# Delta rule inputs scaled on GpSimd, with undrained barriers, a later bank wait and two new orders

## The reference

```
x = x + L0 linear attention;   x = x + L0 FFN
x = x + L1 causal attention (16 heads);   x = x + L1 FFN (16 small experts with group routing, one shared)
x = x + L2 gated delta rule;   x = x + L2 FFN (ternary weights, gelu)
x = x + L3 mixer (attention, short convolution, halting steps, top-2 experts);   x = x + L3 FFN (top-2 of 8 experts)
```

```
xp = silu(conv4(x @ in_proj.T) + conv_b)
q = l2norm(xp @ Wq.T per head);  k = l2norm(xp @ Wk.T per head);  v = xp @ Wv.T
alpha, beta = mean over a head of sigmoid(xp @ W.T + b)
```

## Time and profile before

| | us |
|---|---|
| runs, three | 1912.32, 1925.83, 1933.3 |
| median of the runs | 1925.83 |
| profiled execution, device time | 1933.14 |
| its span in the profile | 1931.3 |
| PE busy | 1542.5 (80%) |
| DVE busy | 1153.2 (60%) |
| ACT busy | 849.0 (44%) |
| POOL busy | 569.4 (29%) |

### The profile page before, as it was taken

The page is one execution under the profiler, slowest core; times in us unless marked ns, Lnnn a source line. Parts: engine busy times, 40 slices in busy tenths (PEclk is TensorE's granted clock), DMA queues, the critical chain, the costliest instruction groups (busy, mean ns, idle before and its releaser), DMA issues. The chain is left out here.

```text
span 1931.3 us, 46920 instructions
## 1 busy us (share of the span) xinstructions
PE 1542.5 (80%) x16703; PEld 1135.5 (59%) x16703; DVE 1153.2 (60%) x3234; ACT 849.0 (44%) x1633; POOL 569.4 (29%) x782
## 2 busy tenths in 40 slices
PE   5779799999878887789997868788889589431992
PEld 3646566666455665568886545455555389331992
DVE  5755577777467656545653457687877344464344
ACT  2422355565511114434442325466666378201783
POOL 4111011111111112432220321113333446376464
PEclk9979799999989998889997888699998589755996
DMA  4000222222079500000000100222322044121334
GB/s 180 1 1 1 67 58 56 59 57 59 6 229 325 189 1 1 0 3 3 4 3 2 67 1 1 66 66 73 82 70 61 25 113 132 68 88 43 88 92 149
DMA packets 84685, 125.00 MB, mean 65 GB/s; under 512 B 17328, under 2 KB 70576, under 8 KB 82928
## 3 DMA queue, kind: packets, MB, share of 16 engines
q1 hardware_dynamic: 75824, 104.30, 18.5%
q0 software_dynamic: 8640, 17.78, 2.6%
HBM read 67.47 MB, written 55.59 MB: 64 GB/s over the span
## 5 line engine op out<-in xcount | busy, mean ns | idle before, releaser
L1559 DVE TENSOR_REDUCE small<-ps 128x8 f32<-128x1024 f32 (+1 forms) x256 | 312.0, 1224 | 108.8 <-PE ps L1339 70.4
L1482 ACT ACTIVATE scr<-ps 128x1024 f32<-128x1024 f32 x256 | 262.4, 1025 | 212.1 <-PE ps L1314 120.8
L244 POOL TENSOR_TENSOR rstd<-vare,neghalf 128x4 f32<-128x4 f32 (+1 forms) x72 | 63.3, 879 | 414.2 <-DVE vare L223 413.7
L1352 PE MATMUL ps<-scr 128*32 128x256 f32 x2048 | 171.7, 409 | 0.2 <-ACT scr L1482 0.2
L2906 POOL DMA_INDIRECT results<-scr x142 | 136.4, 960 | 98.1 <-DVE scr L2893 49.8
L1301 PEld LDWEIGHTS ps<-scr_r 32*128 32x128 f32 x1024 | 81.3, 193 | 140.0 <-issue 72.6
L2840 PE MATMUL ps<-scr 128*128 128x128 f32 x1136 | 153.0, 279 | 0.0
L1301 PE MATMUL ps<-scr_r 32*128 32x256 f32 x1024 | 134.7, 341 | 22.7 <-ACT scr L1482 12.5
L1332 PE MATMUL ps<-scr_r 32*128 32x256 f32 x1024 | 136.4, 348 | 10.1 <-DMA scr_r<-scr_r 5.6
L2840 PEld LDWEIGHTS ps<-scr 128*128 128x128 f32 x1136 | 141.6, 196 | 0.0
L2886 DVE TENSOR_TENSOR scr<-ps,scr 128x256 f32<-128x256 f32 x142 | 60.3, 425 | 130.3 <-ACT scr L2877 124.7
(11 more groups left out here) (416 smaller groups left out, 3495.7 us busy)
## 6 DMA issues: line engine op xcount, KB each, us to landing
scr_r<-scr_r SPq DMA_DIRECT2D x512, 64.0 KB
rows_m<-kinds SPq DMA_DIRECT2D x8, 2064.0 KB, 30.1
rows_f<-kinds SPq DMA_DIRECT2D x8, 2064.0 KB, 73.7
scr<-results SPq DMA_DIRECT2D x32, 256.0 KB
scr<-rows_m SPq DMA_DIRECT2D x71, 64.5 KB
scr<-rows_f SPq DMA_DIRECT2D x71, 64.5 KB
scr<-in_l3m SPq DMA_DIRECT2D x1, 3072.0 KB, 9.9
results<-scr POOLq DMA_INDIRECT x142
```

The lines of the kernel that those rows point to most:

```text
L244: pool.tensor_tensor(k.rstd[:, 0:self.J], k.vare[:, 0:self.J], k.neghalf[:, 0:self.J], ALU.pow).then_inc(self.e["rstd_ready"].sem, 1)
L1352: ins = pe.matmul(ps[32 * r:32 * r + 32, 6, col:col + 256], Vp[:, c % 2, 4 * kt + r, at:at + 32], PT[:, g % 2, r, kt * 256:kt * 256 + 256] ...
L1482: act.activation(PT[:, g % 2, 2 * x:2 * x + 2, :], ps[:, 4:6, :], ACT.Exp).then_inc(e["prob_ready"].sem, 1)
L1559: dve.tensor_reduce(nf[:, half, 0:blocks, at:at + 2].rearrange("p q a -> p a q"), ps[:, 2 * (p % 2):2 * (p % 2) + 2, :].rearrange("p a (q ...
```

## The change

GpSimd, not VectorE, scales queries and keys in the delta inputs, right behind its power; the signal `scaled` goes. At the end of four phases (attention with sorting, both sorted experts, `phase_between`) GpSimd increments the barrier's semaphore without a drain. The power in `space` goes. In the routed FFN the wait for bank 6 moves from ahead of gate and up to ahead of the spreading matmuls. The double norm's normalisation, its transposes and their copy come one block later. In linear attention keys and values come ahead of the transposes, on TensorE and on ScalarE.

```diff
--- before.py
+++ after.py
@@ -180,7 +180,11 @@
             if name in ph:
                 ph[name](eng)
             if n < len(self.phases) - 1:
-                eng.drain().then_inc(self.phase_end, 1)
+                if name in ph.get("landed", ()):
+
+                    eng.sem_inc(self.phase_end, 1)
+                else:
+                    eng.drain().then_inc(self.phase_end, 1)
 
                 if name == "sp" and "sp_late" in ph:
                     ph["sp_late"](eng)
@@ -305,7 +309,7 @@
 class TwiceNorm(Norm):
 
 
-    lag = (1, 1, 2)
+    lag = (1, 1, 3)
 
     def __init__(self, k, bank, scale, shift, once):
         super().__init__(k, 4, bank, scale=scale, shift=shift)
@@ -539,10 +543,9 @@
                 sums(it - 1)
             if there(it):
                 queries(it)
+                keys_values(it)
             if there(it - 2):
                 turn(it - 2)
-            if there(it):
-                keys_values(it)
             if there(it - 1):
                 uses(it - 1)
             if there(it - 2):
@@ -564,13 +567,13 @@
         for it in range(NBLK + 3):
             if there(it):
                 feature(it, eq, rq, ps[:, 0, :], "q_ready", "q_read", "phq_ready")
+                four = lambda ap: ap.rearrange("p (b t c) -> p b t c", b=2, t=2)
+                feature(it, four(ek), four(rk), kpart(0), "kv_ready", "k_read", "phk_ready")
             if there(it - 2):
                 wait(act, "o_turned", it - 2)
                 wait(act, "proj_ready", it - 3)
                 act.activation(oT, ps[:, 6, :], ACT.Copy).then_inc(e["oT_kept"].sem, 1)
             if there(it):
-                four = lambda ap: ap.rearrange("p (b t c) -> p b t c", b=2, t=2)
-                feature(it, four(ek), four(rk), kpart(0), "kv_ready", "k_read", "phk_ready")
                 wait(act, "prod_ready", it - 1)
                 act.activation(vb[:, :, 0:128].rearrange("p (b t) c -> p b t c", b=2), kpart(128),
                                ACT.Copy).then_inc(e["v_ready"].sem, 1)
@@ -708,12 +711,6 @@
             else:
                 if begun(it):
                     pe.wait_ge(e["h_ready"].sem, e["h_ready"].at(it - 1, chunks - 1 + c))
-            if c < routed:
-                if c:
-                    pe.wait_ge(e["spread_read"].sem, e["spread_read"].at(it, c))
-                else:
-                    if begun(it):
-                        pe.wait_ge(e["spread_read"].sem, e["spread_read"].at(it - 1))
             x = k.XT[:, bass.ts(it, BLK)]
             s = 2 * (c % 2)
             ins = pe.matmul(ps[:, s, :], gate[:, c * P:(c + 1) * P], x, start=True, stop=True)
@@ -722,6 +719,10 @@
             ins.then_inc(e["gu_ready"].sem, 1)
             if c < routed:
                 pe.wait_ge(e["widened"].sem, e["widened"].at(it, c + 1))
+                if c:
+                    pe.wait_ge(e["spread_read"].sem, e["spread_read"].at(it, c))
+                elif begun(it):
+                    pe.wait_ge(e["spread_read"].sem, e["spread_read"].at(it - 1))
                 for j in range(4):
                     ins = pe.matmul(ps[:, 6, j * P:(j + 1) * P], wide[:, it % 2, c, j * P:(j + 1) * P],
                                     k.w["const"]["ident"], start=True, stop=True)
@@ -765,7 +766,7 @@
                 ln.pe_route(pe, it)
         if lag:
 
-            staged_by((2,), (0,), pe, NBLK, lambda it, stages: body(it, lambda s: stages() if s == 0 else None), late)
+            staged_by((3,), (0,), pe, NBLK, lambda it, stages: body(it, lambda s: stages() if s == 0 else None), late)
         elif routed:
             written_out(pe, NBLK, body, late, 2)
         else:
@@ -811,7 +812,7 @@
         if route:
             route.act(act)
         if lag:
-            staged_by((2,), (0,), act, NBLK, lambda it, stages: body(it, lambda s: stages() if s == 0 else None), late)
+            staged_by((3,), (0,), act, NBLK, lambda it, stages: body(it, lambda s: stages() if s == 0 else None), late)
         else:
             def open_it():
                 act.wait_ge(consts.e["consts_made"].sem, consts.e["consts_made"].at(0))
@@ -1611,7 +1612,7 @@
             sort.share(dve)
 
     front(Opening(project, high, low, heads_out))
-    k.add_phase(pool=pool, pe=pe, act=act, dve=dve, sp=sp)
+    k.add_phase(pool=pool, pe=pe, act=act, dve=dve, sp=sp, landed=("pool",) if sort else ())
 
 
 def conv_taps(dve, c, x, cw, cb):
@@ -1636,7 +1637,7 @@
 
     nc, ps, cst, w = k.nc, k.ps, k.w["const"], k.w["l2a"]
     e = k.signals(NBLK, xp_ready=1, conv_ready=1, conv_gate=1, xc_ready=1, gate_turned=2, gate_kept=2, means_ready=1,
-                  qk_ready=1, squares=1, qk_kept=1, v_ready=1, v_read=1, norms_ready=1, inverse_norms=1, scaled=1)
+                  qk_ready=1, squares=1, qk_kept=1, v_ready=1, v_read=1, norms_ready=1, inverse_norms=1)
     last = k.signals(1, clamped=1, logs=1, log_sums=1)
     c, sg, xc, gt, sq, n2, rn, mean, bias = k.carve(
         (512,), (512,), (2, 512), (2, 512), (1024,), (16,), (16,), (2, 2), (2,))
@@ -1748,8 +1749,12 @@
     def pool(pool):
         for it in range(NBLK):
             wait(pool, "norms_ready", it)
-            wait(pool, "scaled", it - 1)
             pool.tensor_tensor(rn, n2, k.neghalf[:, 0:16], ALU.pow).then_inc(e["inverse_norms"].sem, 1)
+            pool.drain()
+            wait(pool, "qk_kept", it)
+            rows = heads(qkv[:, tl(it), 0:256])
+            pool.tensor_tensor(rows, rows, spread_last(rn, 64).rearrange("p (t b) d -> p t b d", b=4), ALU.mult)
+            pool.drain()
 
     def dve(dve):
 
@@ -1781,13 +1786,6 @@
             dve.drain()
             dve.tensor_scalar(n2, n2, 1e-24, None, ALU.max).then_inc(e["norms_ready"].sem, 1)
 
-        def scale(it):
-            wait(dve, "inverse_norms", it)
-            wait(dve, "qk_kept", it)
-            rows = heads(qkv[:, tl(it), 0:256])
-            dve.tensor_tensor(rows, rows, spread_last(rn, 64).rearrange("p (t b) d -> p t b d", b=4),
-                              ALU.mult).then_inc(e["scaled"].sem, 1)
-
         for it in range(-1, NBLK):
             if there(it + 1):
                 conv(it + 1)
@@ -1795,9 +1793,6 @@
                 sizes(it)
             if there(it + 1):
                 conv_gated(it + 1)
-            if there(it - 1):
-                scale(it - 1)
-        scale(NBLK - 1)
         wait(dve, "means_ready", NBLK - 1)
         dve.tensor_scalar(alpha, ps[:, 6, 0:64].rearrange("p (t h) -> p t h", h=2), 1e-19, None,
                           ALU.max).then_inc(last["clamped"].sem, 1)
@@ -2688,17 +2683,11 @@
         b, e, o = NBLK - 1, self.e, self.once
         pool.wait_ge(e["places"].sem, e["places"].at(b))
         self.send(pool, b, 0)
-        self.space(pool)
         pool.wait_ge(o["second_named"].sem, o["second_named"].at(0))
         for j in range(4):
             t = 4 * b + j
             pool.indirect_dma_start(self.rows, bass.IndirectOffsetOnAxis(ap=self.place[:, 1, t:t + 1], axis=0),
                                     self.twin[:, j, :], None).then_inc(self.sent[2 + b % 2].sem, 16)
-
-    def space(self, pool):
-
-        two = self.k.two
-        pool.tensor_tensor(two[2][:, 0, :], two[1][:, 0, :], self.k.neghalf[:, 0:4], ALU.pow)
 
     def send(self, pool, b, n, tiles=range(4)):
         for t in tiles:
@@ -2908,7 +2897,7 @@
         for j in range(SORTED - OUT, SORTED):
             landed(pool, j)
 
-    k.add_phase(sp=sp, pe=pe, act=act, dve=dve, pool=pool)
+    k.add_phase(sp=sp, pe=pe, act=act, dve=dve, pool=pool, landed=("pool",))
 
 
 class Gathered:
@@ -2995,13 +2984,11 @@
                 pool.wait_ge(d.e["named"].sem, d.e["named"].at(b - 1))
                 d.send(pool, b - 1, 0)
             if 0 <= b - 2 < NBLK:
-                if b == NBLK + 1:
-                    d.space(pool)
                 pool.wait_ge(d.e["second_named"].sem, d.e["second_named"].at(b - 2))
                 d.send(pool, b - 2, 1)
         d.all_sent(pool)
 
-    k.add_phase(sp=sp, dve=dve, pe=pe, act=act, pool=pool)
+    k.add_phase(sp=sp, dve=dve, pe=pe, act=act, pool=pool, landed=("pool",))
 
 
 def phase_last_rows(k, g, out):
```

## The result

The changed kernel takes 1867.39 us (median of 4 runs, 1866.91 to 1869.51), the kernel before 1929.57 us in the 4 runs beside it (1912.32 to 1936.49). The ratio is 0.969, 95% interval 0.963 to 0.976. The forecast was 1869. Beside the experiments the kernel before takes 1926.75 us (e1 to e4: 23 runs, 1917.06 to 1936.03) and, on a second chip, 1929.03 us (e5 to e8: 14 runs, 1920.41 to 1937.89). One run of e3_lag3, 2250.40 us at a granted clock of 0.66, was in a slower state of the chip, and the medians here are of the other runs.

The account below looks back on a forecast made before the run. TensorE, busy 80% of the span, was taken to bound the kernel where it does not wait for other engines. Terms 17.9 + 15.7 + 14.6 + 7.5 + 1.6 = 57.3 took 1933.14 to 1875.8, as median 1868.5, said 1869; range 1852 to 1891.

Parts of the forecast that it names:

- the five places: Barriers, routed FFN, double norm, linear attention, delta rule's inputs: waits on other engines in the first four, no TensorE gap in the last.
- Barriers and spacing power: Four phase ends: bare increments replace GpSimd's drains and the spacing power goes; 17.9 us off, bounds 1 and 19.
- a busy unit: Last phase: if GpSimd is really occupied as long as the drain, its first addition waits 0.8 us; gain 5.0, not 5.84.
- Rival A: Phase ends: the increment queues behind the drain's work, so barriers give 1 us instead of 17.9; 1886, chance 0.12.
- The later bank wait: Routed FFN: gate and up no longer wait for bank 6's read; 15.7 us off, bounds 8 and 19.5.
- The new wait before the third spread: Routed FFN: VectorE late by about 0.5 us at chunk 2, made up before chunk 3.
- Lag 3: Double norm: normalisation one block later ends VectorE's 3.7 us wait for GpSimd's powers, TensorE becomes the bound; 14.6 us off.
- Linear attention: Keys and values ahead of the transposes close gaps of 1.80 and 1.53 us; 7.5 us off, bounds 2 and 9.
- Scaling: Delta inputs: GpSimd scales at 2.54 us, gain only at the stage's end; 1.6 us off, bounds 3 off and 8 on.
- The lower end of the range: Whole kernel: range starts at 1852; upper bounds of gain (19, 17, 16.5, 9, 3) were said to give 1861.

Follow-up runs that it names:

- e1: Kernel before with GpSimd's bare increments at the four phase ends and without the spacing power, nothing else; 1904.28 us, ratio 0.990.
- e4: Kernel before with keys and values ahead of the turned rows on TensorE, key features ahead of the copy on ScalarE; 1920.55 us, ratio 0.995.
- e5: Kernel before with keys and queries scaled on GpSimd behind its power, nothing else; 1925.32 us beside 1929.03, ratio 0.998.
- e8: Changed kernel plus a last scratch phase timing three VectorE forms alone and beside five GpSimd forms; alone they take 0.69, 0.43 and 0.69 us.
- e3_lag3: Kernel before with lag 3 in the double norm, nothing else; 1913.90 us, ratio 0.993.
- e7: Changed kernel with one small GpSimd power right behind each of the four undrained barriers; 1871.57 us in its one run.
- e10: Changed kernel with GpSimd's drain back at the attention's end alone, on another chip (kernel before 1968.36 us there); 1916.83 us in one run.

## Why the prediction was right

In each of the five places the wait that was to go did go, and the stage gained about what its term said. By the forecast's own terms:

- **Barriers and spacing power, 17.9.** Measured 17.8 alone and 17.5 in the profiled pair. First experts 5.5 and 5.9 (forecast 5.7), phase_between 6.0 and 5.9 with ScalarE last, as forecast (5.2), attention's end 1.95 (2.0). In the second experts and the last phase 4.3 and 3.8 (5.0), and not for my reason: I had a busy unit hold the last phase's first addition for 0.8 us, and e7 shows no busy unit. The addition did come 0.6 us later behind its gather (5.68 us for 5.05), but in e1_barriers, undrained too, it came at 5.12, so the missing drain alone does not make that delay. What is lost in every kernel with four undrained barriers is the 0.7 to 1.1 us at the 217th scatter. Rival A fell with e1. That the sum held is in part luck: it has no term for what a later drain takes, and e10, with one drain back, shows such a term of 6 to 7 us at the end of the program.
- **The later bank wait, 15.7.** Measured 17.4. A steady block went from 23.40 to 21.24 us, 2.16 for my 2.1, and blocks 1 and 2 by 0.92 and 0.93 for my 1.1. The new wait before the third spread was 0.50 us in a steady block, as forecast. The missing 1.7 us are in the first block, which went from 34.84 to 30.77 us where its printed waits were 2.6, and in the last, with 2.9 for 2.1, where no normalisation delays VectorE.
- **Lag 3, 14.6.** Measured 14.5 (14.2 alone): 13.1 up to the eighth first down projection (12.5) and 1.5 behind it (2.1).
- **Linear attention, 7.5.** Measured 10.5 in the profiled pair, 9.4 alone: the largest miss. The steady round gained 1.50 (1.4). I gave the first round with a turn 0.5 and it gained 1.2; and I did not see that one round of the profiled run of before, 9.93 us, carried 1.7 us of half clock.
- **Scaling, 1.6.** Measured 2.5 (2.2 alone). The scaling takes 1.90 us, not 2.54. The nearest row was not the addition of 512 that I doubled but one in the next phase of the kernel before, a GpSimd product of 1024 columns with a broadcast factor:

```profile
809.39 1.90 POOL L1896 TENSOR_TENSOR scr<-w_const,small 128x1024 f32<-128x1024 f32 x1
```

The five terms sum to 57.3, the stages to 62.4, and the profiled span fell by 66.5. Of the rest 3.9 us lie in the untouched work of the attention, where the clock moves the length most. That the median came out 1.6 us from the forecast is in part luck: the terms were 5 us too small, and the median of 1925.83 that they were set against came from three runs and was 3.7 below the 1929.57 of the comparison. The two misses nearly cancel. The lower end of the range has a slip: it adds up the largest gains with 17 for the bank wait, where that part's own bound is 19.5; with it the sum gives 1858 to 1859 instead of 1861, still inside the range.

## What to carry to other kernels

Before a long wait is priced, look for what it is proportional to: four drains of different length and a count would have told that GpSimd's drain charges by the scatters since the last one. When a drain is left out, look at the next one, and at the program's end too: with all four out it took 0.4 us more and nobody waited for it, with three out it took 8.4 us more and the kernel's last phase was 6 to 7 us longer. Where two engines share access, ask which form each instruction has: one with an input in PSUM, or a small power, ran beside the other engine with hardly a loss here; a large SBUF addition on GpSimd did not run beside VectorE's product of two SBUF tiles. And when a kernel's times spread by 1%, cut the trace into stages: the FFN of layer 2 with the old lag repeated to 0.5 us while the attention before the experts moved by 17.

## What the runs showed of the hardware that I had not expected

- GpSimd's drain behind indirect scatters that have all landed takes 0.04 us and 0.082 us for each scatter since its last drain (8, 12, 64 and 71 scatters: 0.70, 1.02, 5.26 and 5.84 us); an increment takes 0.04. The unit is free meanwhile (e7).
- The line ends somewhere above 71: the program's last drain took 9.78 us behind 206 scatters since the drain before it, and 1.78 behind 218, where the 217th had come 1.14 us late.
- A power of 4 or 16 columns on GpSimd delays a VectorE product by at most 0.06 us, but is itself delayed by 0.5 us when it starts second.
- Chips differ by 20 us in each of the sorted experts (114 and 135 us), whose code is the same; why is open.
